# Residual norms cut in four and placed among a shared expert's up products, and the last sums of all tiles taken shared rows first

## The reference

```python
x = x + _layernorm(attention_block(_layernorm(x)))
x = x + _layernorm(experts(_layernorm(x)))

# attention_block(x): q, k, v, gates, scan over time, two norms per head, then
    h = x + out @ Wo
    h2 = _layernorm(h, ln2w, ln2b)
    return h + silu(h2 @ Wgate) * (h2 @ Wval) @ Wout          # 256 -> 1024 -> 256

# experts(x)
    shared = (silu(x @ sw_gate) * (x @ sw_up)) @ sw_down      # 256 -> 704 -> 256
    probs = softmax(x @ router_w.T); top 2 of 8, weights normalised
    routed = sum over the two picked experts of weight * expert(x)   # 256 -> 176 -> 256
    return routed + sigmoid(x @ shared_gate_w)[:, None] * shared
```

## Time and profile before

| | |
|---|---|
| Three runs | 681.04 us median, 680.34 to 682.08 |
| The profiled execution | 681.84 us, of which the span from first to last instruction is 679.9 |
| Granted clock of TensorE, mean | 0.909 of 2.4 GHz |
| Busy: PE, DVE, ACT, POOL | 555.5, 394.5, 241.9, 109.5 us |
| DMA | 45.42 MB moved |

### The profile page before, as it was taken

How to read it: one execution, slowest core, us unless ns; L and a number is a source line. 1 busy time by engine, 2 the same in 40 slices (tenths; PEclk the granted TensorE clock), 3 DMA queues, 4 the chain that set the end, 5 groups by cost and what they waited for, 6 DMA issues and landing times.

```text
span 679.9 us, 7579 instructions
## 1 busy us (share of the span) xinstructions
PE 555.5 (82%) x2332; PEld 414.5 (61%) x2332; DVE 394.5 (58%) x1238; ACT 241.9 (36%) x418; POOL 109.5 (16%) x133
## 2 busy tenths in 40 slices
PE   3843568996599988999998989949789999999390
PEld 1431445775366767877866768837667777776280
DVE  6868554799838998525688544161135555553036
ACT  3701354353555143462124551111211344444022
POOL 1600004000031410020600000400004133334000
PEclk9967669999589997999998989988889999999596
DMA  8950000000100112000100000100342333331703
GB/s 289 401 142 31 0 2 0 1 32 0 62 1 0 41 55 63 1 31 1 63 32 0 1 31 1 64 31 0 96 152 71 96 102 110 110 108 66 262 1 123
DMA packets 30505, 45.42 MB, mean 67 GB/s; under 512 B 3147, under 2 KB 25163, under 8 KB 30123
## 3 DMA queue, kind: packets, MB, share of 16 engines
q1 hardware_dynamic: 25475, 33.99, 15.7%
q0 software_dynamic: 3408, 9.38, 3.8%
q10 hardware_dynamic: 1584, 1.57, 0.8%
HBM read 28.60 MB, written 16.34 MB: 66 GB/s over the span
## 4 chain that ended last, share of the span: by engine, by line
PE 47%; DVE 28%; issue 12%; POOL 6%; ACT 4%; DMA 3%; POOLq 0%; DVEq 0%; ACTq 0%; SPq 0%
PE psum L686 10%; PE psum L651 7%; PE psum L652 7%; PE psum L653 7%; PE psum L712 6%; POOL y_routed L463 5%; PE psum L661 3%; PE psum L761 2%; PE psum L893 2%; DVE rt L925 1%; DVE rt L924 1%; DVE est L944 1%; PE psum L747 1%; DMA YF<-y_routed 1%; PE psum L891 1%
## 5 line engine op out<-in xcount | busy, mean ns | idle before, releaser
L1239 DVE TENSOR_TENSOR SM<-SM,psum 128x512 f32<-128x512 f32 (+1 forms) x56 | 38.0, 683 | 98.2 <-ACT SM L578 98.1
L578 ACT ACTIVATE SM<-psum 128x512 f32<-128x512 f32 (+1 forms) x56 | 33.0, 595 | 141.9 <-PE psum L653 87.4
L454 POOL DMA_INDIRECT x_dispatched<-XN,dest x32 | 32.5, 1017 | 210.3 <-DVE XN L1304 201.7
L686 PE MATMUL psum<-WOU,SM 128*128 128x256 f32 x256 | 60.1, 379 | 0.3 <-DVE SM L1239 0.3
L712 PE MATMUL psum<-WQKV,HT 128*128 128x512 f32 (+1 forms) x128 | 51.8, 557 | 6.8 <-ACT GA L565 3.3
L686 PEld LDWEIGHTS psum<-WOU,SM 128*128 128x128 f32 x256 | 48.0, 189 | 9.3 <-issue 1.4
L844 PE MATMUL psum<-RUP,GX 128*128 x156 | 52.7, 460 | 0.4 <-DVE GX L1319 0.4
L651 PE MATMUL psum<-XTH,supH 128*128 128x512 f32 (+1 forms) x96 | 43.3, 451 | 11.3 <-DVE SM L1239 10.5
L445 POOL TENSOR_TENSOR OG<-QKV,hvec 128x256 f32<-128x256 f32 x16 | 13.4, 840 | 238.8 <-ACT IG L520 220.2
L463 POOL DMA_INDIRECT y_routed<-GO,g_dest x39 | 37.7, 967 | 69.1 <-ACT GO L628 68.5
L712 PEld LDWEIGHTS psum<-WQKV,HT 128*128 128x128 f32 x128 | 26.5, 214 | 30.2 <-issue 25.9
(11 more groups left out here) (252 smaller groups left out, 1158.2 us busy)
## 6 DMA issues: line engine op xcount, KB each, us to landing
XG<-x_dispatched SPq DMA_DIRECT2D x39, 130.0 KB
YF<-y_routed SPq DMA_DIRECT2D x2, 2048.0 KB, 10.7
RUP<-rup SPq DMA_DIRECT2D x1, 2816.0 KB
X<-x SPq DMA_DIRECT2D x4, 512.0 KB, 6.5
x_after_attention<-X SPq DMA_DIRECT2D x4, 512.0 KB, 2.8
XF<-x_after_attention SPq DMA_DIRECT2D x1, 2048.0 KB, 8.3
out<-XF SPq DMA_DIRECT2D x2, 1024.0 KB, 4.7
QKV<-x ACTq DMA_DIRECT2D x3, 512.0 KB
```

Of the source, the lines that this page charges most:

```text
L454: nc.gpsimd.indirect_dma_start(XD[:, :], bass.IndirectOffsetOnAxis(dest[:, i, old + j:old + j + 1], 0), XN[:, j, :], None).then_inc(dispat ...
L578: nc.scalar.activation(SM[0:rows, g % 3, 0:tb], p_pair(n)[0][0:rows, 0:tb], ACT.Silu).then_inc(silu_ready, 1)
L686: last = nc.tensor.matmul(p_down[:, j // 2, (j % 2) * D:(j % 2 + 1) * D], SM[0:rows, g % 3, j * P:(j + 1) * P], weight[0:rows, m, :], star ...
L1239: nc.vector.tensor_tensor(SM[0:rows, g % 3, 0:tb], SM[0:rows, g % 3, 0:tb], p_pair(n)[1][0:rows, 0:tb], ALU.mult).then_inc(hid_ready, 1)
```

## The change

Four things change. (1) `sum` now has three parts: part 1 is the inverse root alone, part 2 the scaling and the add to X. (2) For blocks 1 to 3 the pieces sum 1, sum 2, x2 0 and x2 1 no longer stand in one row ahead of the shared expert of the block before: one follows each of its first four up products. (3) In the last block's shared expert the second pick (choose 2) moves ahead of hid 2. (4) The last sums take the shared rows of all 16 tiles first, before they wait for YF, then the routed rows tile by tile; shared rows of tiles 12 to 15 stay in SH. The numbers in PLACE for blocks 1 to 3 are all new, to fit the new list; of them one row stands here.

```diff
 def _order():
-    def shared(b, at_rank):
+    def shared(b):
         out = []
         for i in range(SMN + 3):
-            out += [("hid", b, i)] if i < SMN else []
-            out += [("sdn", b, i - 3)] if i >= 3 else []
-            out += [("rank", b, 0), ("choose", b, 3)] if i == 2 and at_rank else []
-        return out + [("shout", b, 0)]
+            out += [[]]
+            out[-1] += [("hid", b, i)] if i < SMN else []
+            out[-1] += [("sdn", b, i - 3)] if i >= 3 else []
+        return out + [[("shout", b, 0)]]
+
+    def weave(parts, between):
+        out = []
+        for i, part in enumerate(parts):
+            out += part + between.get(i, [])
+        return out
...
-        order += [("mdn", b, FM - 1), ("sum", b, 0), ("sum", b, 1), ("x2", b, 0), ("x2", b, 1)]
+        order += [("mdn", b, FM - 1), ("sum", b, 0)]
+        norms = {0: [("sum", b, 1)], 1: [("sum", b, 2)], 2: [("x2", b, 0)], 3: [("x2", b, 1)]}
         if b > 0:
-            order += shared(b - 1, False)
+            order += weave(shared(b - 1), norms)
+        else:
+            order += [s for part in norms.values() for s in part]
         order += [("xt", b, 0), ("route", b, 0), ("choose", b, 0)]
-    last = shared(NB - 1, True)
-    return order + last[:1] + [("choose", NB - 1, 1)] + last[1:3] + [("choose", NB - 1, 2)] + last[3:]
+    b = NB - 1
+    return order + weave(shared(b), {0: [("choose", b, 1)], 1: [("choose", b, 2)], 2: [("rank", b, 0), ("choose", b, 3)]})
...
     "pe": [
...
-        [0, 0, 2, 2, 2, 2, 2, 2, 3, 3, 3, 3, 3, 4, 4, 4, 5, 6, 8, 8, 8, 8, 11, 11, 11, 11, 12,
+        [0, 0, 2, 2, 2, 2, 2, 3, 3, 3, 3, 4, 4, 4, 4, 5, 5, 6, 8, 8, 10, 10, 11, 12, 15, 15, 15,
...
+        def sh_tile(n):
+            return SHF[:, n, :] if n < START[NB - 1] else SH[:, n - START[NB - 1], :]
...
-            def total(g):
+            def add_to_tile(n, rows, **flags):
+                return nc.tensor.matmul(f_tile(n), ident[:, :], rows, skip_group_check=True, **flags)
+
+            pe.wait_ge(sf_in, 16)
+            pe.wait_ge(go_ready, NG)
+            for n in range(NT):
+                add_to_tile(n, sh_tile(n), start=n % 2 == 0, stop=False)
+            for g in range(len(FIN)):
                 pe.wait_ge(yf_in[g], 16)
-                if g == 0:
-                    pe.wait_ge(sf_in, 16)
-                    pe.wait_ge(go_ready, NG)
...
                 for n in range(FSTART[g], FSTART[g + 1]):
-                    shared = SHF[:, n, :] if n < START[NB - 1] else SH[:, n - START[NB - 1], :]
-                    nc.tensor.matmul(f_tile(n), ident[:, :], shared, start=True, stop=False)
                     for i in range(2):
-                        last = nc.tensor.matmul(f_tile(n), ident[:, :], YF[:, n, i * D:(i + 1) * D], start=False, stop=i == 1)
-                last.then_inc(sum_psum, 1)
+                        last = add_to_tile(n, YF[:, n, i * D:(i + 1) * D], start=False, stop=i == 1)
+                    last.then_inc(sum_psum, 1)
...
                 if (stage, m) == ("sum", 1):
-                    link(rsqrt(ers[:, 0:nj], eva[:, 0:nj], ers[:, 0:nj], ert[:, 0:nj]))
+                    step(rsqrt(ers[:, 0:nj], eva[:, 0:nj], ers[:, 0:nj], ert[:, 0:nj]))
+                if (stage, m) == ("sum", 2):
+                    settle()
                     for j in range(nj):
...
-                dve.wait_ge(sum_psum, g + 1)
+                dve.wait_ge(sum_psum, FSTART[g + 1])
```

More of the change, by code:

```diff
@@ L167, in f_tile @@
         def f_tile(n):
-            g = max(g for g in range(len(FIN)) if FSTART[g] <= n)
-            j = n - FSTART[g]
-            return psum[:, 4 * (g % 2) + j // 2, (j % 2) * D:(j % 2 + 1) * D]
+            return psum[:, n // 2, (n % 2) * D:(n % 2 + 1) * D]
         def g_bank(stage, i):
@@ L183, in build @@
             XF, SHF, YF, XG, GX, GH, GT, GO, past, moved, g_exp, g_row, g_lim, g_w, g_keep, g_spare, g_to, fst, fmv, fin_r, fin_n = (last_names.enter_context(nc.sbuf_tensor(k, s, F32)) for k, s in (
-                ("XF", [P, NT, D]), ("SHF", [P, NT, D]), ("YF", [P, NT, 2 * D]), ("XG", [P, XRING, XW]), ("GX", [P, 2, C, P]),
+                ("XF", [P, NT, D]), ("SHF", [P, START[NB - 1], D]), ("YF", [P, NT, 2 * D]), ("XG", [P, XRING, XW]), ("GX", [P, 2, C, P]),
                 ("GH", [P, 2, EI]), ("GT", [EK, 2, EC, P]), ("GO", [P, ORING, D]), ("past", [P, NG, E]), ("moved", [P, NG, E]),
@@ L386, in _ @@
             sp.dma_start(XF[:, :, :], XS.rearrange("(j p) d -> p j d", p=P)).then_inc(xf_in, 16)
-            sp.dma_start(SHF[:, 0:START[NB - 1], :], SS[0:START[NB - 1] * P, :].rearrange("(j p) d -> p j d", p=P)).then_inc(sf_in, 16)
+            sp.dma_start(SHF[:, :, :], SS[0:START[NB - 1] * P, :].rearrange("(j p) d -> p j d", p=P)).then_inc(sf_in, 16)
             sp.wait_ge(table_ready, 1)
@@ L643, in _ @@
                     n = FSTART[g] + j
-                    nc.scalar.activation(SHF[:, n, :], f_tile(n), ACT.Identity, bias=shift[:, j:j + 1],
+                    nc.scalar.activation(sh_tile(n), f_tile(n), ACT.Identity, bias=shift[:, j:j + 1],
                                          scale=r[:, j:j + 1]).then_inc(fin_normed, 1)
@@ L879, in _ @@
                         group("down", i - 1)
-            def total(g):
-                pe.wait_ge(yf_in[g], 16)
-                if g == 0:
-                    pe.wait_ge(sf_in, 16)
-                    pe.wait_ge(go_ready, NG)
-                if g >= 2:
-                    pe.wait_ge(fin_normed, FSTART[g - 1])
+            def add_to_tile(n, rows, **flags):
[5 more added lines that the diff above has]
+            for g in range(len(FIN)):
+                pe.wait_ge(yf_in[g], 16)
                 for n in range(FSTART[g], FSTART[g + 1]):
-                    shared = SHF[:, n, :] if n < START[NB - 1] else SH[:, n - START[NB - 1], :]
-                    nc.tensor.matmul(f_tile(n), ident[:, :], shared, start=True, stop=False)
                     for i in range(2):
-                        last = nc.tensor.matmul(f_tile(n), ident[:, :], YF[:, n, i * D:(i + 1) * D], start=False, stop=i == 1)
-                last.then_inc(sum_psum, 1)
-            for g in range(len(FIN)):
-                total(g)
+                        last = add_to_tile(n, YF[:, n, i * D:(i + 1) * D], start=False, stop=i == 1)
+                    last.then_inc(sum_psum, 1)
         @block.vector
@@ L1044, in finish @@
                     dve.wait_ge(fin_normed, n + 1)
-                    nc.vector.tensor_tensor(XF[:, n, :], XF[:, n, :], SHF[:, n, :], ALU.add).then_inc(out_ready, 1)
+                    nc.vector.tensor_tensor(XF[:, n, :], XF[:, n, :], sh_tile(n), ALU.add).then_inc(out_ready, 1)
             def table():
```

## The result

| | before | after |
|---|---|---|
| Median of the runs | 680.69 us (680.18 to 682.08, 4 runs) | 649.58 us (648.78 to 650.06, 4 runs) |
| Span of the profiled execution | 679.9 | 647.6 |
| Mean granted clock | 0.909 | 0.910 |
| Busy: PE, DVE, ACT, POOL | 555.5, 394.5, 241.9, 109.5 | 552.8, 392.1, 237.5, 108.8 |

The ratio is 0.9528, with a 95% interval of 0.9502 to 0.9554. The forecast was 648. The kernel after was measured once more beside the last experiments: 648.21 us (647.15 to 649.64, 5 runs). The kernel before, run beside each set of them, stood at 680.8 to 681.1.

A forecast was written before the change was run, and what follows sets the result against it. TensorE was taken as the bound, only its empty and lower-clock time counting. Terms 12.5 + 6.5 + 4.0 + 2.2 + 1.2 + 7.1 = 33.5 us off 681.84 gave 648.3, 647.5 by the median, stated as 648; range 641 to 661.

The forecast's parts named there:

- Block 3's norms: Block 3's last norms: TensorE's 10.5 us wait before the third hid product and 2.0 us of lower clock go; 12.5 us less.
- Blocks 1 and 2: Shared stage in block 1 and block 2: waits and slow products at wo and centring go; 6.5 + 4.0 us less.
- Block 0 to 1: Between blocks 0 and 1: q 0 covers routing's wait for XTL, q 1 keeps the clock, 1.6 given back; 2.2 us less.
- Choose 2: Last shared stage: rank product's 2.79 us wait goes, sixth product waits some 2.4 instead; -2.8 or about 0, taken as 1.2 less.
- The end: Last sums: shared rows done in the wait for YF, which shortens to some 4.5 us, 2.3 of clock kept; 7.1 us less.
- The price beside it: Shared stage of block 0: twelve moved GpSimd multiplies slow VectorE's root steps; 0 in the sum, 1.6 us in the range.
- rival 2: GpSimd beside VectorE: its 1.6 us fall where TensorE has no lead; 650 us, chance 0.05.
- Rival 1: VectorE in order: multiplies queue behind waiting attention steps, only block 3 and the end pay; about 661.4 us, chance 0.20.
- rival 3: The clock: woven stages break TensorE's work into short pauses that hold it at 1.2 GHz; some 700 us, chance 0.03.
- rival 4: The change doesn't do what it says: queues give the same waits around block 3's norms; same time, 681, chance 0.02.
- the mean clock: Sign over the whole span: the prediction would be wrong if the mean clock is not above 0.91.

The follow-up runs named there:

- row3: Kernel after with block 3's four norm pieces back in one row ahead of block 2's shared expert: 659.20 us.
- only3: Kernel before with only block 3's norms in pieces among the up products: 669.34 us.
- again: Kernel after, unchanged, measured once more on the same chip as the last experiments: 648.21 us.
- row1: Kernel after with block 1's four norm pieces in one row ahead of block 0's shared expert, attention steps left in place: 655.72 us.
- row2: Kernel after with block 2's four norm pieces in one row ahead of block 1's shared expert, attention steps left in place: 659.19 us.
- tail_back: Kernel after with the old end, each tile's shared row behind the wait for YF: 654.39 us.
- choose_back: Kernel after with choose 2 of the last block behind hid 2 again: 650.04 us.
- warm: Kernel after with shared rows of tiles 0 to 9 taken twice, keeping TensorE busy in the wait for YF: 646.76 us.
- mix: Kernel after with the 24 routing products of blocks 0 to 2 issued three at a time among the next block's first up product: 651.49 us.
- all3: Kernel after with ten tiles' shared rows taken twice, last statistics taken by the PSUM bank, and routing products among the first up product: 648.01 us.
- tail_only: Kernel before with the new end alone: 674.13 us.

## Why the prediction was right

- **Block 3's norms** (12.5; 12.4). Both parts held: the wait of 10.5 us, and 2.0 us of clock. Row3 and only3 show it with either surroundings. The walk with pieces and multiplies, made from differences of starts in the earlier trace rows, was right to 0.3 us. The rule that I drew from it was not: I wrote that only a piece with its multiply of over 5.6 us would break the cover. That lead is there once. Each of the first three pieces with its multiply took 2.7 to 4.2 us, against 2.8 for a product, so together they eat it up. By the same walk, pieces that took 5.0 us each with their multiplies would end multiply 0 in time (5.4 against 5.6) and multiply 1 at 10.4, where TensorE needs it at 8.4. The true margins were 1.0 and 1.1 us.
- **Blocks 1 and 2** (10.5; 9.3). The waits went as priced and more: 7.1 us less empty, for 6.7 in the sum. The slow part was mis-sized: I credited 2.71 + 1.15 = 3.9 us of clock, and TensorE's busy time fell by 2.2 only. The step that failed is that the clock lost before wo and the centring product would simply come back. It did there, but two other places lost more than before. Behind block 1's routing the kernel after is at half clock from 305 to 309, about 1.7 us lost (an estimate from windows of one microsecond), where the kernel before had nothing; a wait of 0.29 us stands there that it had not. Behind block 2's routing the wait grew from 1.36 to 2.01 us and the loss from about 3.4 to 5.0.
- **Block 0 to 1** (2.2; 1.0). The number lies near by luck. I credited 0.4 us of waits (2.01 gone, 1.6 given back) and 1.8 of clock at q 1. The trace has 1.6 us less waiting (2.01 and 1.63 gone, of which I had not named the second, and 2.15 new before xt) and 0.6 us more busy time: q 1 does run at full clock (2.74 us), but the half clock came again behind the routing and slowed the first up product in its place. In the nine traces of this code this stretch takes 76.4 to 76.6 us where no lower clock follows the routing (again, row1, row2, tail_back) and 78.7 to 79.4 where it does. Against this trace of the kernel before (80.48 us) the change is so worth 1.0 to 1.8 or about 4 us here, and 2.2 is neither.
- **Choose 2** (1.2; 1.6, and 1.8 in choose_back). The pause moved to the sixth product, 2.19 us for 2.4. But the 1.2 was a mean of two cases, and neither came as written: the sixth product had waited 0.80 us before, so TensorE's waits became 1.1 us less, not 0.4, and in this trace the clock fell behind the new pause as it had behind the old one.
- **The end** (7.1; 6.85, 6.7 net of the later landing). The pause came to 4.42 us for 4.5, and warm shows that keeping 2.3 us for the clock was right (2.4).
- **The price beside it** and rival 2 did not arise. The Trainium skill has it (GPSIMD Engine Reference, 1. Specifications) that GpSimd and VectorE contend where VectorE reads two SBUF inputs. The trace of the kernel before agrees, 0.60 against 0.19 us. In the kernel after the roots of this stage (256.1 to 258.3, and 278.1 to 280.4) end before the first of the twelve multiplies begins, and each of their steps took 0.16 or 0.17 us:

```profile
280.29 0.16 DVE L960 SCALAR_TENSOR_TENSOR x2n<-emv,x2r 128x4 f32<-128x4 f32 x1
```

```profile
281.58 0.72 POOL L456 TENSOR_TENSOR OG<-QKV,hvec 128x256 f32<-128x256 f32 x1 [43.44 <-ACT IG L531]
```

- **Rival 1** is excluded by the 9.3 us of blocks 1 and 2, **rival 3** by the clock of 1.00 in block 3's woven stage and 0.96, as before, in those of blocks 1 and 2 (its price was wrong too: 648 + 83 is 731, not some 700), **rival 4** by row3.
- One of the signs that I gave was badly chosen: the mean clock is 0.910, not above 0.91, though every term came. A mean over the span falls when full-speed time is removed with the waits: by the two means about 124 and 117 us were at half, so of the 32.3 us that went only about 7 were.
- 1.26 us before 171.47 were not predicted, and are not shown to be the change's: the same point lies at 170.6 to 171.8 us in the three traces with the old places and at 169.4 to 171.6 in the eleven with the new.

## What to carry to other kernels

When a row of dependent small steps sits on one in-order engine in front of the work that frees another engine's buffers, cut it in pieces and put one unit of the freeing work behind each. The other engine's lead, here two products or 5.6 us, is what the pieces draw on together: add up pieces and units, and hold each sum against the moment at which the other engine needs that buffer. In block 3 the smallest margin was 1.0 us. Places and pieces belong together: with the order tuned for the woven list, a row in one block cost 7.7 or 13.6 us, more together than the 9.3 that both gained. And before moving narrow work out of the way of a wide product, look at what it covered: in the mix it was hiding a second wait twice as long.

## What the runs showed that I had not expected

**The clock falls behind narrow products, mostly where a short wait stands ahead of them.** In the kernel after, the 24 routing products of 10 columns of block 1 start at 302.79, behind a wait of 0.29 us, run at full speed for the first 2.5 us, and come ahead of a drop to half (1.2 GHz), though TensorE is busy throughout from 303 to 310. Two windows of the kernel after, then the same places of the program in mix, where these products are spread among wide ones:

```profile
303.00:304.00 1.00, 1.00 (x11) 1.00 (x10) 0.97 (x2) 0.98 (x2) 0.00 (x0) 1.00 0.00 0
307.00:308.00 1.00, 1.00 (x4) 0.71 (x3) 0.02 (x1) 0.93 (x2) 0.00 (x0) 0.50 0.00 0
```

```profile
303.00:304.00 1.00, 1.00 (x9) 0.93 (x8) 0.97 (x2) 0.00 (x0) 0.00 (x0) 1.00 0.00 0
307.00:308.00 1.00, 1.00 (x7) 0.83 (x6) 0.70 (x2) 0.95 (x2) 0.00 (x0) 1.00 0.00 0
```

Neither mix nor all3 shows a lower clock behind the routing of block 0 or 1. Of the nine other traces with block 1's new places (row1 among them), eight do behind block 1's, and warm does not; each of the nine has a wait of 0.28 to 0.34 us ahead of the row. Mix and all3 have neither the row nor that wait, so they do not tell which of the two matters. The row by itself does not have to lower it: in before, only3 and tail_only the same 24 products stand in a row with no wait ahead, and the clock stays at 1.00 in all three. The kernel before, where the row runs from 298.75 to 301.59:

```profile
302.00:303.00 1.00, 1.00 (x6) 0.81 (x5) 0.32 (x3) 0.61 (x2) 0.00 (x0) 1.00 0.00 0
```

Behind block 0's routing, where no wait stands directly ahead either but one of 2.15 us some 6 us earlier, it falls in five of the nine. A run that keeps the row and takes only the wait away was not made with the new places.

**The same code gets the clock back at other moments.** The stretch from the QKV transposes to block 1's end took 79.44 us in the kernel after and, in its second measurement:

```profile
170.78:247.26 76.48, 70.14 (x299) 51.52 (x299) 62.67 (x177) 36.19 (x52) 16.80 (x20) 0.92 0.10 33
```

There are 299 matmuls in both, and TensorE's busy time differs by 3.2 us. A term of under some 3 us cannot be told from a pair of totals. It has to be read from its own stage, and from more than one trace where the clock is part of it. From totals, 9.6 us for row3 and 4.8 for tail_back looked like failures of terms that their stages confirm.

**YF came later where a packet of instructions fell beside its load.** SP issues both halves at once, and the first sum starts 8.4 us later in the kernel after (605.90 to 614.35), where TensorE works for 4.0 of them. In warm and all3, where it works for 8.3 of them, 9.6 us pass (603.83 to 613.42, 607.61 to 617.17). The bytes move about as fast beside a busy TensorE as beside an idle one; the last figures of these windows are the share of the DMA engines and GB/s, first of warm, then of the kernel after:

```profile
608.00:610.00 2.00, 2.00 (x11) 1.77 (x10) 0.00 (x0) 0.00 (x0) 0.00 (x0) 1.00 1.06 395
```

```profile
612.00:614.00 2.00, 0.00 (x0) 0.00 (x0) 0.00 (x0) 0.00 (x0) 0.00 (x0) 0.63 1.04 400
```

The Trainium skill (SBUF — State Buffer, SBUF: two separate sides) says that a DMA cannot be slowed by a compute operation; the rate agrees. What does go with the delay is another DMA. Each trace has one packet of 16 KB of an instruction queue near this load, and where it falls beside the load it takes 1.0 to 1.1 us. Below, the half microsecond in which it starts, in warm (609.30 to 609.80), in the kernel after (617.90 to 618.40) and in the kernel before (647.00 to 647.50); the columns are packets, MB and the share of the 16 DMA engines:

```profile
q8 instruction: 1, 0.02, 12.6%
```

```profile
q8 instruction: 1, 0.02, 13.7%
```

```profile
q8 instruction: 1, 0.02, 15.2%
```

| Packet starts, us after the issue | Traces | First half lands | Second half lands |
|---|---|---|---|
| 15.3 to 15.7, behind the load | before, only3, tail_back (old end) | 8.2 to 8.3 | 13.1 to 13.2 |
| 12.0 to 12.5, in the second half | nine with the new end | 8.2 to 8.4 | 14.3 to 14.5 |
| 5.5, in the first half | warm, all3 | 9.5 | 14.4 |

So whatever lands after the packet lands 1.1 to 1.4 us later, in all fourteen traces. TensorE's own work fits less well: it works twice as long beside the load in warm as in the kernel after, and the second half lands no later. The packet moved only where TensorE's list at the end changed, which fits its holding instructions of TensorE; no run moved it by itself, so this is an order of events and not an experiment. In warm it takes back half of what the kept clock gives. In the kernel after only the second half is late, and TensorE has no wait there.
